# A layer norm finished before the projection: shift per row in the scaling pass, bias folded into the weights

## The reference

```
zn = layer_norm(z, ln_in_w, ln_in_b)
a = m * sigmoid(zn @ w_ag + b_ag) * (zn @ w_ap + b_ap)
b = m * sigmoid(zn @ w_bg + b_bg) * (zn @ w_bp + b_bp)
p = einsum('bikc,bjkc->bijc', a, b)
x = layer_norm(p, ln_out_w, ln_out_b) @ w_z + b_z
g = sigmoid(zn @ w_g + b_g)
return x * g
```

## Time and profile before

| | |
|---|---|
| time, median of 3 runs (lowest, highest) | 1846.29 us (1845.77, 1848.07) |
| the profiled execution: time, and its span | 1851.94 us, 1850.2 us |
| PE busy | 1605.2 us (87%) |
| DVE busy | 1426.6 us (77%) |
| ACT busy | 1212.6 us (66%) |
| POOL busy | 1010.1 us (55%) |

### The profile page before, as it was taken

The page is one execution under the profiler, slowest core; times in us unless marked ns, Lnnn a source line. Parts: engine busy times, 40 slices in busy tenths (PEclk is TensorE's granted clock), DMA queues, the critical chain, the costliest instruction groups (busy, mean ns, idle before and its releaser), DMA issues. The chain is left out here.

```text
span 1850.2 us, 38459 instructions
## 1 busy us (share of the span) xinstructions
PE 1605.2 (87%) x10716; PEld 1054.3 (57%) x10716; DVE 1426.6 (77%) x4779; ACT 1212.6 (66%) x2950; POOL 1010.1 (55%) x1722
## 2 busy tenths in 40 slices
PE   5999989986859879879999989997849999999987
PEld 3444459775745468645555568885744444444442
DVE  6999950555969979889999821567959999999986
ACT  5999956332749879748888855334846766666641
POOL 5888840344767700057777710456865666666642
PEclk9999999999989989979999999998958999999999
DMA  4687764678885364047888774888965666666642
GB/s 129 192 225 201 216 194 138 213 263 270 313 313 162 115 245 174 2 139 233 236 249 245 212 210 127 258 284 280 379 195 158 188 182 189 179 185 186 176 134 84
DMA packets 387912, 373.41 MB, mean 202 GB/s; under 512 B 155040, under 2 KB 303264, under 8 KB 385696
## 3 DMA queue, kind: packets, MB, share of 16 engines
q1 hardware_dynamic: 342688, 304.32, 55.2%
q10 hardware_dynamic: 45056, 67.13, 10.6%
HBM read 186.80 MB, written 150.99 MB: 183 GB/s over the span
## 5 line engine op out<-in xcount | busy, mean ns | idle before, releaser
L563 PE MATMUL cp_pv<-conv_weight,cp_zt 64*128 64x320 f32 x2048 | 363.8, 463 | 33.7 <-DVE cp_b_stage L355 24.0
L1554 DVE TENSOR_TENSOR ex_xe<-ex_spread,ex_xd 128x512 f32<-128x512 f32 x512 | 317.3, 681 | 20.4 <-PE ex_spread L1835 17.4
L353 DVE SCALAR_TENSOR_TENSOR a_res<-cp_pv,cp_mask,cp_sig 128x64 f32<-128x64 f32 x1024 | 263.5, 322 | 50.9 <-ACT cp_sig L512 42.3
L512 ACT ACTIVATE cp_sig<-cp_pv 128x384 f32<-128x384 f32 x512 | 243.1, 490 | 68.6 <-PE cp_pv L563 64.5
L563 PEld LDWEIGHTS cp_pv<-conv_weight,cp_zt 64*128 64x128 f32 x2048 | 175.2, 186 | 165.7 <-issue 142.1
L1851 PE MATMUL ex_po<-ex_xe,ex_expert 128*64 128x512 f32 x1024 | 249.5, 608 | 0.0
L773 PE MATMUL cp_pv<-a_res,cc_room 128*128 128x256 f32 x896 | 209.6, 384 | 14.0 <-DMA cc_room<-b_scratch 10.8
L492 ACT ACTIVATE cp_xn<-cp_x,cp_lift,cp_rstd 128x64 f32<-128x64 f32 x512 | 195.7, 438 | 36.8 <-POOL cp_lift L440 36.8
L773 PEld LDWEIGHTS cp_pv<-a_res,cc_room 128*128 128x128 f32 x896 | 171.3, 197 | 37.8 <-DMA cc_room<-b_scratch 18.7
L885 POOL TENSOR_TENSOR cc_p<-cc_p,cc_room 128x512 f32<-128x512 f32 x64 | 103.7, 1620 | 147.3 <-DVE cc_room L854 143.6
L1699 ACT ACTIVATE ex_xn<-ex_x,ex_lift,ex_rstd 128x64 f32<-128x64 f32 x480 | 171.5, 429 | 17.7 <-POOL ex_lift L1619 17.7
(11 more groups left out here) (207 smaller groups left out, 3317.9 us busy)
## 6 DMA issues: line engine op xcount, KB each, us to landing
gate_scratch<-cp_sig SPq DMA_DIRECT2D x128, 256.0 KB, 2.8
b_scratch<-cp_b_stage SPq DMA_DIRECT2D x128, 256.0 KB, 3.9
cc_room<-b_scratch SPq DMA_DIRECT2D x128, 256.0 KB, 3.0
ex_xd<-ex_xt SPq DMA_DIRECT2D x256, 128.0 KB, 2.6
cp_x<-in_x SPq DMA_DIRECT2D x64, 256.0 KB, 3.4
cc_room<-gate_scratch ACTq DMA_DIRECT2D x64, 256.0 KB, 4.3
cc_p<-in_x SPq DMA_DIRECT2D x64, 256.0 KB, 4.7
after_conv<-cc_p ACTq DMA_DIRECT2D x64, 256.0 KB, 3.7
```

The costliest lines, as they stand in the source:

```text
L353: dve.scalar_tensor_tensor(a_res[:, h, :, row], bank[:, h, 3 * C:4 * C], mask_sb[:, h, row:row + 1], sig[u.mod(2)][:, 0, h, i, :], ALU.mul ...
L512: act.activation(sig[u.mod(2)][:, :, :, i, :].rearrange("p k h c -> p h k c"), pv[slot(u, i)][:, :, 0:3 * C].rearrange("p h (k c) -> p h k ...
L563: pe.matmul(pv[slot(u, i)][:, h, 0:COLS], zt[u.mod(2)][half, i * P:(i + 1) * P], weight[half, :], start=True, stop=True).then_inc(v_made, 1)
L1554: dve.tensor_tensor(xe[u.mod(2)][:, :, h, i * P:(i + 1) * P], pb[k][:].rearrange("p (e t) -> p e t", e=EP), xd[u.mod(8)][:, h, i * P:(i + ...
```

## The change

The rows are normalised in full by the scaling pass: to p times `rstd` a row's constant is added. So the weights no longer centre, and the bias can be part of them.

- `refine` gets two more GpSimd instructions per quad: `lift` is set to `numbers[:, 1:2]` (the constant 1) minus sum-mean times `rstd`. `ROOTS`, the count of semaphore steps per quad, goes from 4 to 6; `stats` gets a second buffer, and `measure` waits for the quad before last to be refined instead of the last one's `halve`.
- `scale` becomes one `tensor_scalar` for each row, (p * rstd) + lift with both scalars read per partition: 8 instructions of 128x64 in the lower half, 4 in the upper half.
- `scale_rest` on ScalarE has the same 4 instructions, with Identity and a bias in place of Copy.
- `project` loses the bias matmul; its four matmuls start their own accumulation.
- `fold_projection` has one matmul of 64 columns instead of two, then two `tensor_scalar` of 64x64 into a zeroed `weight_out`; the three-part bias is gone, and OUT goes from 10 to 4. The constant added to every normalised row (the channels' constant sum) makes the offset part of the folded weights.

```diff
         def fold_projection(half):
             if half == 0:
                 dve.wait_ge(pack_out_in, 16)
-                dve.tensor_scalar(fold_out, pack_out[:, 0:P], pack_out[:, 2 * P:2 * P + 1], None, ALU.mult
+                dve.tensor_scalar(fold_out, pack_out[:, 0:P], pack_out[:, P:P + 1], pack_out[:, P + 1:P + 2], ALU.mult,
+                                  ALU.add).then_inc(out_folds, 1)
+                dve.memset(weight_out[:], 0.0).then_inc(out_folds, 1)
+                return
+            dve.wait_ge(out_folded, 1)
+            dve.wait_ge(out_folds, 2)
+            for r in range(2):
+                block_of = slice(r * C, (r + 1) * C)
+                dve.tensor_scalar(weight_out[block_of, block_of], bank_out[block_of, 0:C], 1.0 / C, None, ALU.mult
                                   ).then_inc(out_folds, 1)
...
-            was = bank_out[:, P:P + C]
-            for q in range(3):
-                dve.tensor_copy(part[q], was).then_inc(out_folds, 1)
...
-            for q in range(3):
-                ins = dve.tensor_copy(bias3[32 * q:32 * q + 32, :], part[q][32 * q:32 * q + 32, :])
-            ins.then_inc(out_folds, 1)
...
-            pe.matmul(po[n % 3], ones3[:], bias3[:].unsqueeze(1).to_broadcast([P, SR, C]),
-                      start=True, stop=True)
             for j in range(PAIRS):
                 ins = pe.matmul(po[n % 3][:, j * 2 * C:(j + 1) * 2 * C], pt(n)[:, j * P:(j + 1) * P], weight[:],
-                                start=False, stop=True, skip_group_check=True)
+                                start=True, stop=True)
...
-            if n % 4 == 0 and n:
-                dve.wait_ge(halved, n // 4)
+            if n % 4 == 0 and n >= 8:
+                dve.wait_ge(refined, (n // 4 - 1) * ROOTS)
...
-            here = dve_rows(n)
-            dve.tensor_tensor(pn(n)[:, 0:here, :], p_rows(n, 0, here),
-                              over(rstd[n // 4 % 2][:, n % 4, 0:here], C), ALU.mult).then_inc(pn_made, 1)
+            for i in range(dve_rows(n)):
+                ins = dve.tensor_scalar(pn(n)[:, i, :], p_rows(n, i, 1)[:, 0, :], rstd[n // 4 % 2][:, n % 4, i:i + 1],
+                                        lift[n // 4 % 2][:, n % 4, i:i + 1], ALU.mult, ALU.add)
+            ins.then_inc(pn_made, 1)
...
+            to = lift[quad % 2][:].rearrange("p n i -> p (n i)")
+            pool.wait_ge(refined, quad * ROOTS + 4)
+            pool.tensor_tensor(to, stats[quad % 2][:, :, :, 1].rearrange("p n i -> p (n i)"),
+                               rstd[quad % 2][:].rearrange("p n i -> p (n i)"), ALU.mult).then_inc(refined, 1)
+            pool.wait_ge(refined, quad * ROOTS + 5)
+            pool.tensor_tensor(to, numbers[:, 1:2].to_broadcast([P, QUAD]), to, ALU.subtract).then_inc(refined, 1)
...
-                ins = act.activation(pn(n)[:, i, :], p_rows(n, i, 1)[:, 0, :], ACT.Copy,
-                                     scale=rstd[n // 4 % 2][:, n % 4, i:i + 1])
+                ins = act.activation(pn(n)[:, i, :], p_rows(n, i, 1)[:, 0, :], ACT.Identity,
+                                     scale=rstd[n // 4 % 2][:, n % 4, i:i + 1], bias=lift[n // 4 % 2][:, n % 4, i:i + 1])
```

More of the change, by code:

```diff
@@ L71, in over, with constants @@
     return ap.unsqueeze(len(ap.shape)).to_broadcast(list(ap.shape) + [n])
[L78 to L83, removed]
-        for q in range(3):
-            dve.memset(ones3[32 * q:32 * q + 1, :], 1.0).then_inc(rows_made, 1)
+def constants(block, ident, numbers, made):
     @block.gpsimd
@@ L154, in conv_project @@
 def conv_project(nc, m, block, x, mask, packed, packed_out, a_res, b_dram, gate_dram, ident, numbers, weight, weight_out,
-                 bias3, room_at, load_chunk, parts=None, before=None):
+                 room_at, load_chunk, parts=None, before=None):
     KINDS = 5
@@ L190, in conv_project @@
     pack, fold = cut(0, P + 2 + COLS), cut(512, P)
-    pack_out, fold_out, offset = cut(768, 2 * P + 2 + C), cut(1152, P), cut(1280, P)
-    rest = [cut(1408 + C * q, C) for q in range(2)]
-    part = [cut(1536 + C * q, C // 2).bitcast(BF16) for q in range(3)]
+    pack_out, fold_out = cut(768, P + 2 + C), cut(1152, P)
     bank_out = pv[2][:, 1, :]
@@ L570, in fold_projection @@
         def fold_projection():
[L571 to L574, removed]
+            pe.wait_ge(out_folds, 1)
+            pe.matmul(bank_out[:, 0:C], fold_out, pack_out[:, P + 2:], start=True, stop=True).then_inc(out_folded, 1)
         def step(s):
@@ L637, in chunk_loads, with conv_combine @@
     return b_in, chunk_used, buffer, load_chunk
-def conv_combine(nc, m, block, x, a_res, gate_dram, out, ident, ones3, numbers, weight, bias3, ptile, room, banks, done,
-                 chunks):
+def conv_combine(nc, m, block, x, a_res, gate_dram, out, ident, numbers, weight, ptile, room, banks, done, chunks):
     CHUNKS = C // CH
@@ L648, in conv_combine @@
     LAST = H * STEPS
-    ROOTS = 4
+    ROOTS = 6
     LEAD = 6
@@ L655, in conv_combine @@
     b_in, chunk_used, buffer, load_chunk = chunks
-    stats = m.sb("stats", [P, 4, SR, 3])
+    stats = [m.sb(f"stats{q}", [P, 4, SR, 3]) for q in range(2)]
+    lift = [m.sb(f"lift{q}", [P, 4, SR]) for q in range(2)]
     half_var = m.sb("half_var", [P, QUAD])
@@ L830, in halve @@
                 dve.wait_ge(refined, quad * ROOTS)
-            dve.tensor_scalar(half_var[:], stats[:, :, :, 2].rearrange("p n i -> p (n i)"), 0.5 / C, 0.5e-5,
+            dve.tensor_scalar(half_var[:], stats[quad % 2][:, :, :, 2].rearrange("p n i -> p (n i)"), 0.5 / C, 0.5e-5,
                               ALU.mult, ALU.add).then_inc(halved, 1)
@@ L1936, in pack_projection @@
 def pack_projection(w):
[L1938 to L1946, removed]
+    packed = np.zeros((P, P + 2 + C), np.float32)
+    packed[0:C, 0:P] = np.tile(C * np.eye(C, dtype=np.float32) - 1.0, (1, 2))
+    packed[0:C, P] = w["ln_out_w"]
+    packed[0:C, P + 1] = w["ln_out_b"]
+    packed[C, P + 1] = 1.0
+    packed[0:C, P + 2:] = w["w_z"]
+    packed[C, P + 2:] = w["b_z"]
     return packed
@@ L1994, in build @@
             weight_out = both.enter_context(nc.sbuf_tensor("weight_out", [P, H * C], F32))
[L1995 removed]
             big = both.enter_context(nc.sbuf_tensor("a_res", [P, P, N], F32))
[L1997 removed]
+            PTILE, ROOMS, SMALL, OVER = N * C * 4, 6 * 2048, 1824, 1920
             low = (nc.sbuf_base + 31) // 32 * 32
@@ L2016, in conv @@
                                                a[f"L{layer}_conv_pack_out"], a_res, b_dram, gate_dram, ident, numbers,
-                                               weight, weight_out, bias3, low + PTILE, chunks[3], **given)
-                    conv_combine(nc, m2, block, x, a_res, gate_dram, y, ident, ones3, numbers, weight_out, bias3, ptile,
-                                 room, banks, done, chunks)
+                                               weight, weight_out, low + PTILE, chunks[3], **given)
+                    conv_combine(nc, m2, block, x, a_res, gate_dram, y, ident, numbers, weight_out, ptile, room, banks, done, chunks)
             conv(0, a["x"], t0, a["L0_conv_pack"],
-                 lambda m, block: constants(block, ident, ones3, numbers, m.sem("made"), m.sem("rows_made")))
+                 lambda m, block: constants(block, ident, numbers, m.sem("made")))
             with Scope(nc, "si", low, low + PTILE - OVER) as m:
```

20 lines of the change are left out of this document (2 added, 18 removed).

## The result

The changed kernel is slower: 1976.28 us (median of four runs, 1972.41 to 1981.90) against 1847.18 us (1845.77 to 1850.10), a ratio of 1.069, 95% interval 1.067 to 1.072. Its profiled execution took 1973.76 us with a span of 1972.0; that is 121.82 more than the profiled execution of before. In what follows two executions that were far slower than the rest of their kernel, 1905.88 and 6687.06 us, are left out.

What follows compares the result with a forecast made beforehand. VectorE's step was taken to bound the upper half, the loop through the gate's transfer the lower. 1851.9 - 4 + 48 + 68 = 1964, less 5.65, gave 1958 us; range 1888 to 2020.

Steps and rivals of the forecast that it cites:

- The meeting: In every step GpSimd's add gets in behind the scale's first instruction; the others wait, about 1.05 us; chance 0.70.
- The rival in which the run keeps its way: VectorE's scale instructions go through and GpSimd's add waits: 1908 us; chance 0.13.
- the one without a meeting: Scale instructions of 64 elements need little of what GpSimd's add holds, so neither is held: 1891 us; chance 0.10.
- the one that has the run cheaper than one instruction: VectorE's four short scale instructions take 0.31 us for the old scale's 0.52: 1829 us; chance 0.04.
- The instructions' own price: VectorE's scale: 0.2225 us per instruction, up to 0.05 more where strided; eight 1.78 for 0.61, four 0.89 for 0.52.
- Lower halves: Steps of the lower half go from 3.82 to 4.6 us, for 62 steps: +48 us, bounds +30 and +73.
- Upper halves: Upper half: 48 steps at +1.3 us and 16 first and last ones at +0.4: +68 us, bounds +46 and +99.
- The opening: TensorE's first transpose waits less for the bias parts, 2.6 us in the first convolution, 1.4 in the second: -4 us.
- At nothing: The missing bias matmul, ScalarE's bias (11 us without cover by idle time) and two new GpSimd instructions per quad change nothing.
- The sum: Whole kernel: 1851.9 - 4 + 48 + 68 = 1964, less 5.65 for the median of the runs: 1958 us.
- A sign against it that came: TensorE's clock falling below 0.96 while it waits longer would show the prediction wrong.

Runs made afterwards that it cites:

- the run with the small add: Changed kernel with GpSimd's residual add on one row of eight, 128x64 in place of 128x512: 1891.67 us, ratio 1.022.
- the first experiment: Changed kernel with VectorE's scale alone put back to one tensor_tensor, the rest of the change kept: 1852.46 us, ratio 1.002.
- The moved wait: Kernel before, with TensorE waiting for the fold ahead of its first write into the bank the fold reads, not its first transpose: 1842.07 us, ratio 0.998.

## Why the prediction was right

**The meeting.** Shown. The first of a run passes, the add starts 0.16 behind it, and the next is held until it ends. In the trace of the changed kernel 119 of the 128 runs have an instruction of more than 1 us; it ends 0.05 to 0.07 us behind the end of an add. In 92 runs it is the second; in most of the others the fourth, which meets an add behind a refinement. Taking the add away (1891.67), putting it behind the run (1906.65) and making the same gap in the old scale (1924.63) each move the time as this says. The rival in which the run keeps its way falls with the runs of 2.82 and 2.06; the one without a meeting falls as a forecast, though its 1891 is what the kernel takes once the add is small; the one that has the run cheaper than one instruction falls with 1.12 for four and 0.52 for the old scale. The Trainium skill (SBUF — State Buffer, "SBUF: two separate sides", under "Who interferes with whom") says that a VectorE instruction with at most one SBUF input, outside the modes that use two ports, does not contend with GpSimd. The traces agree: beside an add the statistics stay at 0.86 and the gate, one of whose inputs is in PSUM, at 0.67. The run, the half variance and the cut tensor_tensor are held; in which mode the first two run no trace shows.

**The instructions' own price.** 0.2225 each, and up to 0.05 more where strided: four take 1.12 with nothing beside them, for 0.98 in the earlier trace rows. Right.

**Lower halves.** +48 predicted, +46.4 measured; a step 4.6 and 4.57. That the two lie so close is partly luck, since the measured loss is known to 46 to 57 only. VectorE is busy for 4.27 of a step, near the 4.44 of the prediction's own sum for it. The loop through the gate's transfer is still near: with the run free it alone gives 4.10 to 4.14 (127.07 and 128.42 us in 31 steps, by the windows of the run with the small add).

**Upper halves.** +68 predicted, +77.5 measured: the term that was too small. A step in the middle costs 3.46 for 2.05, 1.41 more and not 1.3, since the add behind a refinement holds a run too and does not fall into the statistics. And the first and last steps of a half don't pay 0.4 but 0.9: the eleven outside the twenty took 33.74 (102.89 - 69.15) for some 23.8 (64.81 - 20 x 2.05). In the last steps, which have no statistics, where GpSimd's adds set the pace before (4.22 for three), a step is 2.59 now:

```profile
579.24 2.06 DVE L825 TENSOR_SCALAR a_res<-a_res,cc_rstd,cc_lift 128x64 f32<-128x64 f32 x4
579.40 1.32 POOL L869 TENSOR_TENSOR cc_p<-cc_p,a_res 128x512 f32<-128x512 f32 x1 [1.27 <-DVE a_res L832]
...
581.83 2.06 DVE L825 TENSOR_SCALAR a_res<-a_res,cc_rstd,cc_lift 128x64 f32<-128x64 f32 x4
```

**The opening.** -4 predicted; TensorE's wait fell by 3.5 (11.9 to 8.4). That this came off the total is not shown: the first experiment, which keeps it, was no faster than before. The moved wait brought 4, but it takes TensorE's whole wait for the fold away, which the shorter fold doesn't.

**At nothing.** The bias matmul is nothing. ScalarE's bias and the two GpSimd instructions are nothing only under the run's cover, as said of the first with 11 us; without it they are some 1.9 and 2.8 us an upper half, 9.4 in all. Of the second the step was wrong: that a quad's constants are needed two steps later holds for VectorE, but ScalarE already waited 14.9 us for `rstd` in the kernel before.

**The sum.** 46.4 + 77.5 - 3.5 is 120.4 of the 121.82 between the two profiled executions, for 112 predicted. The rest of the 18 us between 1958 and 1976.28 is that I took 5.65 off for the median, while the changed kernel's profiled execution lies 2.5 under its own.

**A sign against it that came.** The prediction was to be wrong, too, if TensorE's clock fell below 0.96. The granted clock of the lower halves did fall, to 0.89 and 0.90. It explains little of the loss: the two upper halves had 0.96 and 0.85 and took 102.89 and 103.92 us, the twenty steps of 3.46 had 1.00, and in the lower halves a slower TensorE can cost no more than the 18.5 us in which VectorE was not busy (9.63 and 8.90).

## What to carry to other kernels

Before one instruction is cut into several, look at what another engine starts meanwhile. Here one instruction that had started went through, and the first gap between several let the other engine in for a whole instruction of its own. Two thirds of the loss (85 of 129 us) came from that, and 70 of the 129 were had back with one wait that puts the other engine's work beside instructions that it doesn't hold; that kernel is still 3% slower than the one before. And a gain of the opening should be tried by itself: moving one wait brought one, without the new arithmetic.

## What the runs showed of the hardware that was not expected

- One cut is enough: two tensor_tensor with an add beside them take 1.60 where one took 0.59.
- Turns: with the add cut in two, one instruction of the run ends between its halves, and two instructions of a run are held for half an add each (0.78 at most; 1.32 with the add whole). GpSimd's halves are not seen to wait in turn: 0.73 at the median, 0.82 at most.
- A GpSimd tensor_tensor of 64 elements, 0.32 to 0.36 us long at the median, costs the run next to nothing (no instruction of L825 longer than 0.41), while one of 512 holds for all of its 1.3. That is no sign that the small one holds nothing: an instruction that starts 0.01 behind it takes 0.36 for 0.30 and ends 0.05 after it, as behind a whole add. It is over before it can cost more.
